# An expert stage with 39 tiles in place of 40, and a feed-forward with three up products a step and two up pieces rounded early

## The reference

```python
# layer 0, first part: top-2 of 8 experts, chosen by the context
scores_topk, idx_topk = top_k(context @ Wg + bg, 2)
h = relu(layernorm(x) @ W1[e] + b1[e]);  y = h @ W2[e] + b2[e]     # 256 -> 1024 -> 256
x = x + sum over the two chosen experts of weight * y
# layer 0, second part: top-1 of 8 experts with 512 places each
# layer 1, first part: attention over the context
# layer 1, second part: gated feed-forward, with values rounded to integers of 16 bits
x = act_qdq(layernorm(x))                     # act_qdq: scale = max|x| / 32767, round, times scale
up = act_qdq(x @ deq(w_up).T)                 # 256 -> 768
gate = act_qdq(x @ deq(w_gate).T)             # 256 -> 768
gate = act_qdq(gate * fixed_qdq_u16(sigmoid(gate)))
o = act_qdq(gate * up)
out = o @ deq(w_down).T                       # 768 -> 256
```

## Time and profile before

| | |
|---|---|
| time, three runs | 1570.85, 1574.60, 1572.52 us; median 1572.52 |
| the profiled execution | 1573.39 us, its span 1571.7 us |
| busy in the span | TensorE 82%, VectorE 74%, ScalarE 53%, GpSimd 30% |
| mean granted clock of TensorE | 0.90 of full speed |
| tiles of the first expert stage | 40, the first transposed rows at 96.7 us, the last at 514.4 us |
| sigmoid steps | VectorE from 1325.5 to 1421.7 us |

### The profile page before, as it was taken

One profiled execution on the slowest core, in us unless ns is written; L12 is line 12 of the kernel. 1 busy time (PEld: TensorE's weight loads), 2 busy tenths in 40 slices (PEclk: granted clock), 3 DMA queues, 4 the chain that ended last, 5 costly groups with the idle time before them and its releaser, 6 DMA issues. The chain is left out here.

```text
span 1571.7 us, 31820 instructions
## 1 busy us (share of the span) xinstructions
PE 1283.2 (82%) x10494; PEld 1043.0 (66%) x10495; DVE 1159.7 (74%) x2040; ACT 840.5 (53%) x1282; POOL 472.0 (30%) x491
## 2 busy tenths in 40 slices
PE   6989999999999772999935999999997498750087
PEld 3458888888888631888834888888887254220076
DVE  2869865555656466996527999999996696998844
ACT  4856533333333231663304667676763667877664
POOL 3234755545554303355321223223223000000000
PEclk9999999999999985999975889998986699995599
DMA  9887633323232275673234010000000101337211
GB/s 320 309 260 216 155 52 53 46 49 51 44 54 38 30 235 164 184 215 52 35 65 145 21 28 20 27 27 20 27 15 1 40 1 41 144 124 259 75 52 57
DMA packets 108871, 147.32 MB, mean 94 GB/s; under 512 B 17136, under 2 KB 84720, under 8 KB 106992
## 3 DMA queue, kind: packets, MB, share of 16 engines
q1 hardware_dynamic: 87280, 116.31, 22.5%
q0 software_dynamic: 21504, 29.83, 11.4%
HBM read 92.62 MB, written 53.49 MB: 93 GB/s over the span
## 5 line engine op out<-in xcount | busy, mean ns | idle before, releaser
L734 ACT ACTIVATE top_x_all<-top_h_ps,top_b1T 128x256 f32<-128x256 f32 x448 | 184.5, 474 | 303.9 <-PE top_h_ps L580 296.1
L580 PE MATMUL top_h_ps<-top_xT_hi,top_w_lo 128*128 128x256 f16 x896 | 245.3, 274 | 1.2 <-issue 1.2
L578 PE MATMUL top_h_ps<-top_xT_hi,top_w_hi 128*128 128x256 f16 x896 | 245.4, 274 | 0.9 <-issue 0.9
L579 PE MATMUL top_h_ps<-top_xT_lo,top_w_hi 128*128 128x256 f16 x896 | 245.4, 274 | 0.0
L596 PE MATMUL top_y_ps<-top_w_hi,top_x_all 128*128 x896 | 244.2, 273 | 0.2 <-DVE top_x_all L933 0.2
L598 PE MATMUL top_y_ps<-top_w_hi,top_x_all 128*128 x896 | 244.2, 273 | 0.0
L597 PE MATMUL top_y_ps<-top_w_lo,top_x_all 128*128 x896 | 244.2, 273 | 0.0
L931 DVE CAST top_x_all<-top_x_all 128x512 f16<-128x512 f32 x224 | 98.1, 438 | 150.0 <-ACT top_x_all L734 146.3
L933 DVE TENSOR_TENSOR top_x_all<-top_x_all 128x512 f16<-128x512 f32 x224 | 155.8, 695 | 7.7
L387 POOL DMA_INDIRECT x_sum<-top_x_all,top_row_of_slot x56 | 96.2, 1718 | 178.7 <-DVE top_x_all L945 155.9
L1742 PE MATMUL ffn_ps<-ffn_dT_hi,ffn_yT 128*128 128x256 f16 x192 | 53.8, 280 | 91.1 <-DVE ffn_yT L2022 91.1
(11 more groups left out here) (321 smaller groups left out, 3118.3 us busy)
## 6 DMA issues: line engine op xcount, KB each, us to landing
top_staged<-in_L_xattn_W SPq DMA_DIRECT2D x32, 512.0 KB
top_staged<-in_L_ffn_w SPq DMA_DIRECT2D x32, 512.0 KB
up_raw<-ffn_u_all SPq DMA_DIRECT2D x48, 256.0 KB, 2.1
ffn_yT<-up_raw SPq DMA_DIRECT2D x12, 1024.0 KB, 4.7
kv_rows<-top_w_lo SPq DMA_DIRECT2D x32, 256.0 KB, 4.3
attn_kv_in<-kv_rows SPq DMA_DIRECT2D x32, 256.0 KB, 2.6
top_w_lo<-in_ctx SPq DMA_DIRECT2D x4, 1024.0 KB, 10.3
top_x_all<-in_x SPq DMA_DIRECT2D x4, 1024.0 KB, 12.0
```

The lines of the kernel that those rows point to most:

```text
L578: nc.tensor.matmul(out, hi, xT_hi[p][:, c, :], start=(c == 0), stop=False)
L579: nc.tensor.matmul(out, hi, xT_lo[p][:, c, :], start=False, stop=False)
L580: last = nc.tensor.matmul(out, lo, xT_hi[p][:, c, :], start=False, stop=(c == DC - 1))
L734: last = nc.scalar.activation(h32[:, fc * R:(fc + 1) * R], h_ps[:, b, q * R:(q + 1) * R], ACT.Relu, bias=b1T[:, bass.ds(e * FC + fc, 1)], ...
```

## The change

In the expert stages the number of tiles is no longer rounded up to a multiple of four: the first stage has 39, the second still 16. Q counts the last, possibly short group, and REST is its number of tiles (3 and 4). The written-out last group runs over REST tiles on TensorE and VectorE; ScalarE writes out the last tiles from 2 * (M - 1) on, with M = NT // 2; GpSimd's last tiles start at the same number as before and end one earlier.

In the feed-forward three up products are taken out in each of the steps 0 to 15 and none in the steps 16 to 23. The reduction of up's maxima moves into step 16 and its scale into step 17. ScalarE rounds up piece 0 in step 20 and up piece 1 in step 22. After the gated value's scale ScalarE's order is gated piece 0, gated piece 1, up piece 2, gated piece 2, up piece 3 and so on. TensorE's and SyncE's lists in this stage stay as they are.

```diff
@@ -128,7 +128,6 @@
     if capacity is None:
 
         NT = (choices * tokens + E * (R - 1)) // R
-        NT += -NT % 4
     else:
         NT = E * capacity // R
     NS = 2 * NT
@@ -275,9 +274,10 @@
         s_added = [sem(f"y{p}_added") for p in range(2)]
 
         M = NT // 2
-        Q = NT // AHEAD
+        Q = -(-NT // AHEAD)
+        REST = NT - AHEAD * (Q - 1)
         HEAD = 2
-        assert NT % AHEAD == 0 and HEAD * AHEAD >= E
+        assert HEAD * AHEAD >= E
         block = ctx.enter_context(nc.Block())
 
         @block.sync
@@ -437,7 +437,7 @@
             with pool.Fori(1, Q - 2) as q:
                 for i in range(AHEAD):
                     add_and_gather(q, i)
-            for j in range(NT - 2 * AHEAD, NT):
+            for j in range(AHEAD * (Q - 2), NT):
                 add_and_gather(j // AHEAD, j % AHEAD, j + EARLY < NT)
 
         def w1_at(w, e, dc, fc):
@@ -601,13 +601,13 @@
 
 
 
-            def tiles(q, experts_split, more=True):
+            def tiles(q, experts_split, n=AHEAD, more=True):
                 first_tile = isinstance(q, int) and q == 0
                 e_before = None if first_tile else expert(AHEAD * q - 1)
-                for i in range(AHEAD):
+                for i in range(n):
                     m, p = 2 * q + i // 2, i % 2
                     e = expert(AHEAD * q + i)
-                    if more or i + 1 < AHEAD:
+                    if more or i + 1 < n:
                         transpose_in(q, i + 1)
                     if not experts_split:
                         pe.wait_ge(s_split, (e + 1) * CPE)
@@ -627,9 +627,9 @@
             pe.wait_ge(s_split, E * CPE)
             with pe.Fori(HEAD, Q - 1) as q:
                 tiles(q, True)
-            e = tiles(Q - 1, True, more=False)
+            e = tiles(Q - 1, True, REST, more=False)
             for fc in range(FC):
-                layer2(M - 1, 1, e, fc)
+                layer2((NT - 1) // 2, (NT - 1) % 2, e, fc)
 
         def split_hi(act, e):
             for c in range(CPE):
@@ -747,9 +747,10 @@
                 for p in range(2):
                     x_high(m + p, 1 - p)
                     hidden(m, p, 2 * m + p)
-            x_high(M - 1, 1)
-            hidden(M - 1, 0, NT - 2)
-            hidden(M - 1, 1, NT - 1)
+            for j in range(2 * (M - 1), NT):
+                if j + 1 < NT:
+                    x_high((j + 1) // 2, (j + 1) % 2)
+                hidden(j // 2, j % 2, j)
 
         def split_lo(dve, e):
             for c in range(CPE):
@@ -965,13 +966,13 @@
                 tiles(q, False)
             with dve.Fori(HEAD, Q - 1) as q:
                 tiles(q, True)
-            for i in range(AHEAD):
-                m, p, j = M - 2 + i // 2, i % 2, NT - AHEAD + i
-                if i + 1 < AHEAD:
+            for i in range(REST):
+                j = AHEAD * (Q - 1) + i
+                if i + 1 < REST:
                     x_low(Q - 1, i + 1)
-                hidden_split(m, p)
-                result(m - 1 + p, 1 - p, j - 1)
-            result(M - 1, 1, NT - 1)
+                hidden_split(j // 2, j % 2)
+                result((j - 1) // 2, (j - 1) % 2, j - 1)
+            result((NT - 1) // 2, (NT - 1) % 2, NT - 1)
 
 
 def this(engine, semaphores, m, p):
@@ -1531,6 +1532,9 @@
     NP = TG * IC
     BANKS = 4
     UB = 4
+    UP_A_STEP = 3
+    UP_STEPS = NP // UP_A_STEP
+    UP_EARLY = (UP_STEPS + 4, UP_STEPS + 6)
     PAIRS = T // 2
     SIG_ROUND = 192.0
     SIG_TOP = 65535.0 / 65536.0
@@ -1624,6 +1628,9 @@
         def gate_at(g, c):
             return flat[:, g * GW + c * N:g * GW + (c + 1) * N]
 
+        def ups(i):
+            return range(UP_A_STEP * i, min(NP, UP_A_STEP * (i + 1)))
+
         def step(i):
             return flat[:, i * CB:(i + 1) * CB]
 
@@ -1820,27 +1827,29 @@
                     act.wait_ge(s_g["product"], i - SB + 1)
                 A.activation(sig[i % SB], low16(step(i)), ACT.Sigmoid, scale=scale[:, 1:2]).then_inc(s_g["sigmoid"], 1)
 
+            def round_up(i):
+                act.wait_ge(s_later[i % LB], 16 * (i // LB + 1))
+                A.activation(later[:, i % LB, :], later[:, i % LB, :], ACT.Identity, bias=round_c[:],
+                             scale=to_int[:, 2:3]).then_inc(s_o["up_rounded"], 1)
+
             act.wait_ge(s_scale, 2)
             round_gate(0)
             for i in range(STEPS):
                 if i + 1 < STEPS:
                     round_gate(i + 1)
                 sigmoid(i)
-                for n in (2 * i, 2 * i + 1):
+                for n in ups(i):
                     evict_up(n)
-
-            def round_up(i):
-                act.wait_ge(s_later[i % LB], 16 * (i // LB + 1))
-                A.activation(later[:, i % LB, :], later[:, i % LB, :], ACT.Identity, bias=round_c[:],
-                             scale=to_int[:, 2:3]).then_inc(s_o["up_rounded"], 1)
+                if i in UP_EARLY:
+                    act.wait_ge(s_scale, 3)
+                    round_up(UP_EARLY.index(i))
 
             def round_gated(i):
                 A.activation(wide_step(i), wide_step(i), ACT.Identity, bias=round_c[:], scale=to_int[:, 3:4]).then_inc(s_o["rounded"], 1)
 
-            act.wait_ge(s_scale, 3)
-            round_up(0)
             act.wait_ge(s_scale, 4)
-            for i in range(WIDE):
+            round_gated(0)
+            for i in range(1, WIDE):
                 round_gated(i)
                 if i + 1 < WIDE:
                     round_up(i + 1)
@@ -1983,15 +1992,17 @@
                 if i > 0:
                     gated_max(i - 1)
                 gated(i)
-                for n in (2 * i, 2 * i + 1):
+                if i == UP_STEPS:
+                    dve.wait_ge(s_um, NP)
+                    V.tensor_reduce(largest[:, BIG_UP:BIG_UP + 1], maxes[:, 1, :], AX_X, ALU.max).then_inc(s_big, 1)
+                if i == UP_STEPS + 1:
+                    dve.wait_ge(s_red, 3)
+                    new_scale(2, unit[:, 0:1])
+                    V.nop().then_inc(s_scale, 1)
+                for n in ups(i):
                     dve.wait_ge(s_ev, NP + n + 1)
                     V.tensor_reduce(maxes[:, 1, n:n + 1], u_out[n % UB], AX_X, ALU.max, apply_absolute_value=True).then_inc(s_um, 1)
-            dve.wait_ge(s_um, NP)
-            V.tensor_reduce(largest[:, BIG_UP:BIG_UP + 1], maxes[:, 1, :], AX_X, ALU.max).then_inc(s_big, 1)
             gated_max(STEPS - 1)
-            dve.wait_ge(s_red, 3)
-            new_scale(2, unit[:, 0:1])
-            V.nop().then_inc(s_scale, 1)
             dve.wait_ge(s_g["max"], STEPS)
             V.tensor_reduce(largest[:, BIG_GATED:BIG_GATED + 1], step_max[:, 0:STEPS], AX_X, ALU.max).then_inc(s_big, 1)
             dve.wait_ge(s_red, 4)
```

## The result

The changed kernel takes 1558.85 us (median of 5 runs, 1555.87 to 1561.71) against 1572.44 us (1568.84 to 1574.60). The ratio is 0.9909, with a 95% interval from 0.9894 to 0.9925, so 14.3 us less by the ratio, 11.8 to 16.7 by its interval. The forecast was 1559.5 us, 13.0 us less.

What follows compares the result with a forecast made beforehand. No engine bounds the whole program: TensorE bounds the first expert stage, VectorE the feed-forward's sigmoid steps. 10.9 + 0.3 + 1.8 = 13.0 us less than the median 1572.52 gives 1559.5 us; range 1557.3 to 1562.7 (forecast's own 1558 to 1562, chance 0.77).

Steps and rivals of the forecast that it cites:

- The tile: First expert stage: one tile fewer saves TensorE's time for a tile, 10.9 us (bounds 10.8 and 11.0).
- The table: Whole-table operations on VectorE: two columns fewer save 0.07 us in each of four, 0.3 us in all (bounds 0 and 0.4).
- Three up products a step: Feed-forward steps 0 to 15: VectorE's work only reordered, 4.65 us a step, costed at nothing; 2.3 us to spare for sigmoids.
- Up's scale in steps 16 and 17: Feed-forward: the moved small work still costs VectorE 1.2 us, as before; step 17's 2.86 us covers the all-reduce.
- One cover: Loads of up pieces: out some 17 us sooner, first needs 4.7 us, against VectorE's step 20 some 12 us after up's last maximum.
- The end: After the last sigmoid step: second wide product starts 8.6 us after VectorE's last step work, not 10.4; gain 1.8 us (1.0 to 2.1).
- A: Rival, sigmoid steps: early rounding or a waiting copy holds back a sigmoid, up to 2 x 2.0 us; 1561.3 to 1563.5; chance 0.11.
- C: Rival, three-product steps: TensorE at 1.2 GHz, 16 steps lose 49 us, about 1609 us, slower than before; chance 0.03.
- The rule on depth-cycling: Skill's rule: short waits round PSUM banks swing the clock between two levels, so the third up product might not fit a step.
- D: Rival, first expert stage: the removed tile was covered, so only 2 us come, 1570.5 us; chance 0.01.
- B: Rival, behind the first stage: the clock's slow stretches fall elsewhere, 2 or 3 us better or worse, 1556.5 to 1562.5; chance 0.08.

Runs made afterwards that it cites:

- the feed-forward alone: Only the feed-forward's part of the change, against the kernel before, with 40 tiles kept: ratio 0.9977 (0.9964 to 0.9990), 3.6 us less.

## Why the prediction was right

**The tile.** Predicted 10.9 us and 0.3 for the table, 11.2 together. The stage means differ by 553.8 - 542.4 = 11.4 us, and three more tiles give (542.4 - 508.9) / 3 = 11.2 us each. From the first steady copy on, without the table and the scatter ahead of it, one tile is 358.14 - 347.13 = 11.0 us, and three more are 11.1 each. With TensorE busy 104.91 of 105 us beside these, its own time is the price and there is no cover. The tail on buffer 0 costs nothing: from the last copy to the next stage it takes as long as the tail on buffer 1.

**The table.** 2.82 to 2.76 us for the operation, as worked out; 0.3 us in all wasn't shown by itself: the mean start of the steady tiles moved from 195.6 to 195.3 us, but single profiles with the same table differ by up to 2.8 us there.

**Three up products a step.** Costed at nothing, and it cost nothing: 4.65 us a step, VectorE full, 2.3 us to spare for the sigmoid, as worked out. The point where it stops was tried: at four products TensorE is nearly full and nothing is lost, at six it sets the step.

**Up's scale in steps 16 and 17.** 1.1 us of VectorE's time moved, none added, and the wait covered. I took the all-reduce as under 1.24 us by the rows; it took 0.72 us in place of 0.35. The cover of one step held it, with 2.0 us left (1387.63 to 1389.59).

One cover was worked out at the wrong engine. I set the loads of up against step 20 as VectorE reaches it, some 12 us after the last up maximum. But it is ScalarE that rounds piece 0, and it had run ahead: it was at its step 20 at 1390.18 (1390.53 less the 0.35 of waiting), 6.4 us after VectorE had issued that maximum (1383.76), and waited there for the scale. The loads went out 8.6 us before that, and the first of the four to land took 4.9 us:

```profile
1381.57 2.02 SPq L1660 DMA_DIRECT2D ffn_yT<-up_raw  x4
```

The wait cost nothing, because ScalarE was over two steps ahead of VectorE. The loads start 20.1 us sooner after the first sigmoid rounding than before (71.1 us in place of 91.2), where I had 17.

**The end.** Predicted 1.8 us, measured 1.9 (shown by the trace in the changed kernel and in the feed-forward alone), 1.7 of it from the second early piece and 0.2 from the rest. I had 0.1 for the rest. Most of the difference is the moved reduction, which I took with its duration of 0.20 us; by starts it costs VectorE 0.12 (1386.61 to 1386.73).

**The sum.** 13.0 us predicted, 14.3 by the ratio (11.8 to 16.7), and 13.3 from the stage means and the steps (11.4 + 1.9). The median of 1558.85 us lies 0.65 below the forecast of 1559.5, well within the scatter of single executions; that the time came so close is in part luck, that the terms did is not.

**The rivals.** A (ScalarE late) is out: VectorE never waits for it in steps 1 to 23. C (the clock) is out at three, four and six products, at 1.00 each time. The rule on depth-cycling in the Trainium skill ("TensorE: Matmul & The Clock Gate"), which would have brought it about, isn't borne out by these rows. (By the sum of C a product of 1.82 us, not 1.85, would have cost the whole gain; nothing rests on it.) D (the tile covered) is out. B has a part: the profiled pair shows 17.5 us, of which 13.1 + 2.3 lie in the changed stages and 2.1 in those whose code is the same. Of the 13.1 us, 2.1 were there before the first steady tile. The execution profiled was the fastest of its five. The means over all profiles show small shifts in stages whose code is the same: the second expert stage is 0.9 us shorter with 39 tiles, with no overlap of the ranges, and attention 1.6 us longer, with overlap. Second stages of another length were what the prediction named as the sign of B. Three profiles with 40 tiles are few, no cause was tried, and the two shifts nearly cancel; this stays open.

## What to carry to other kernels

Where a window shows one engine busy for all but a tenth of a per cent, removing work there pays at that engine's price, and a padding to a round number of loop bodies is such work. Where two engines pass pieces to each other behind a serial point (a scale, a reduction), look at the first two or three pieces one by one: of 1.9 us, 1.7 came from one piece being ready, and a shorter first piece gave nothing until the wait behind it had been filled too, with a third piece rounded early. When the scatter of whole runs is 5 us, measure an effect of 1 us between two events of the trace, and take several profiles before giving a stage the credit for a difference.

## What was not expected of the hardware

The all-reduce over partitions on GpSimd took 0.72 us in the changed kernel, where VectorE's rounding (L1979 there, 1386.73 to 1387.42) and then its maximum (L1988, from 1387.33) ran beside it, and 0.35 us when VectorE stood waiting for it. The other kernels with the changed kernel's order show 0.71 or 0.72 us too.

The kernel before shows which of the two instructions does it. There the same all-reduce had only the maximum beside it, for its whole length (L1979 is that maximum in the kernel before):

```profile
1421.98 1.21 DVE L1979 TENSOR_REDUCE ffn_step_max<-ffn_act_all 128x1 f32<-128x1024 f32 x1
```

```profile
1422.15 0.35 POOL L1671 PARTITION_ALL_REDUCE ffn_reduced<-ffn_largest  x1 [102.54 <-DVE ffn_largest L1990]
```

It took 0.35 us, so the maximum doesn't lengthen it, and what is left is the rounding, which ended 0.21 us before the longer all-reduce did. The Trainium skill ("SBUF — State Buffer", section "SBUF: two separate sides") says that VectorE and GpSimd share a pair of ports as an exclusive lock, held for a whole instruction, when VectorE's instruction is in one of its two-port modes or has two inputs in SBUF. The rows agree with a lock held by the rounding. That the rounding ran in a two-port mode is not shown by any row; it takes 0.60 us by starts for 1024 columns, where the maximum takes 1.13.
